# A two-block image network on one core: which engine takes the positive part and which the square, a second buffer of weighed values, and one form of samples

## The reference

```
x = x + mixer(ln(x))     # sim = relu(xn xn^T) ** 2 over all 3136 tokens; y = sim (x W)
t = t + experts(ln(t))   # 16 experts, the best two of each token, softmax shares
x = x + deformed(ln(x))  # 9 taps; each reads 4 corner rows at positions computed from x; then a 576 -> 64 product
t = t + routed_ffn(ln(t))# the 1567 tokens of largest routing weight get an FFN, weighted
```

## Time and profile before

| | us |
|---|---|
| median of 3 runs | 4409.18 (4400.55 to 4422.35) |
| profiled execution, its own time | 4427.31 |
| its span, first to last instruction | 4425.5 |
| GpSimd busy, in 2608 instructions | 2925.6 |
| TensorE / VectorE / ScalarE busy | 2910.2 / 2435.6 / 1761.2 |

### The profile page before, as it was taken

How to read it: one execution, slowest core, us unless ns; L and a number is a source line. 1 busy time by engine, 2 the same in 40 slices (tenths; PEclk the granted TensorE clock), 3 DMA queues, 4 the chain that set the end, 5 groups by cost and what they waited for, 6 DMA issues and landing times.

```text
span 4425.5 us, 51603 instructions
## 1 busy us (share of the span) xinstructions
PE 2910.2 (66%) x17810; PEld 1891.5 (43%) x17810; DVE 2435.6 (55%) x3747; ACT 1761.2 (40%) x2959; POOL 2925.6 (66%) x2608
## 2 busy tenths in 40 slices
PE   5969687586757786777777676788681357146432
PEld 2434534452446345633465345633460146135321
DVE  6354454744675456655665466655654245345775
ACT  5656466245523562355425552365231112122210
POOL 0040074777777776777767777777777777776770
PEclk8979798678856895678667886589665556555555
DMA  5000214321533132423342144313351325243446
GB/s 123 8 15 9 39 24 102 100 77 50 127 96 96 39 106 82 131 54 97 85 116 77 51 110 111 110 33 107 87 133 47 104 88 131 62 127 91 121 111 120
DMA packets 540746, 375.76 MB, mean 85 GB/s; under 512 B 465872, under 2 KB 470736, under 8 KB 540496
## 3 DMA queue, kind: packets, MB, share of 16 engines
q0 software_dynamic: 110848, 257.07, 20.1%
q1 hardware_dynamic: 429648, 115.40, 12.5%
HBM read 308.79 MB, written 89.41 MB: 90 GB/s over the span
## 4 chain that ended last, share of the span: by engine, by line
POOL 43%; PE 23%; issue 13%; DVE 11%; ACT 4%; DMA 3%; DVEq 2%; SPq 1%; ACTq 0%; POOLq 0%
POOL G L548 28%; PE PS L1689 22%; POOL shared L562 9%; POOL slot_rows L554 6%; DVE G L623 2%; DMA G<-corner_table,index 2%; DVE G L629 1%; DMA out<-experts_w 1%; DVEq L625 1%; DVE small L972 1%; DVE value L631 1%; PE PS L1724 1%; DVE st L590 1%; ACT small L1551 0%; DVE smallc L590 0%
## 5 line engine op out<-in xcount | busy, mean ns | idle before, releaser
L548 POOL DMA_INDIRECT G<-corner_table,index x1800 | 2029.3, 1127 | 681.6 <-issue 537.0
L623 DVE TENSOR_TENSOR G<-G,corner_w 128x768 f32<-128x768 f32 x600 | 541.5, 953 | 678.2 <-DMA G<-corner_table,index 678.1
L1515 ACT ACTIVATE work<-PS 128x768 f32<-128x768 f32 (+2 forms) x800 | 643.2, 822 | 541.9 <-PE PS L1689 277.8
L1689 PE MATMUL PS<-xn 128*128 128x400 f16 (+3 forms) x3200 | 647.9, 346 | 236.0 <-ACT work L1515 229.8
L951 DVE TENSOR_TENSOR work<-work 128x768 f32<-128x768 f32 (+2 forms) x496 | 479.7, 973 | 457.0 <-PE PS L1689 415.3
L554 POOL DMA_INDIRECT slot_rows<-split_a,slot x400 | 485.1, 1213 | 335.1 <-DVE slot L1046 213.5
L562 POOL DMA_INDIRECT shared<-slot_results,slot x400 | 410.1, 1025 | 349.5 <-DMA slot_results<-shared 227.8
L1689 PE MATMUL PS<-work,xm 128*64 128x400 f32 (+3 forms) x3200 | 638.0, 517 | 0.0
L1689 PEld LDWEIGHTS PS<-xn 128*128 128x128 f16 (+1 forms) x3200 | 289.8, 101 | 666.4 <-ACT work L1515 389.2
L1724 PE MATMUL PS<-ident,value 128*128 128x128 f32 x800 | 181.8, 370 | 522.3 <-DVE xq L636 275.5
L1423 ACT ACTIVATE val_cm<-PS 128x512 f32<-128x512 f32 x200 | 119.1, 596 | 694.5 <-PE PS L1724 694.3
(11 more groups left out here) (266 smaller groups left out, 3591.7 us busy)
## 6 DMA issues: line engine op xcount, KB each, us to landing
G<-corner_table,index POOLq DMA_INDIRECT x1800
corner_table<-rows_scratch SPq DMA_DIRECT2D x32, 784.0 KB
shared<-slot_rows SPq DMA_DIRECT2D x32, 512.0 KB, 7.6
slot_results<-shared SPq DMA_DIRECT2D x32, 512.0 KB
corner_table<-G SPq DMA_DIRECT2D x8, 841.0 KB, 10.5
slot_rows<-split_a,slot POOLq DMA_INDIRECT x400
shared<-slot_results,slot POOLq DMA_INDIRECT x400
experts_w<-x_scratch SPq DMA_DIRECT2D x8, 784.0 KB, 6.2
```

What stands on the lines that cost most here:

```text
L548: GP.indirect_dma_start(G[0:rows, n % 2, tap * 4 * C:(tap + 1) * 4 * C], None, tables[b % 2], bass.IndirectOffsetOnAxis(ap=index[0:rows, c ...
L623: V.tensor_tensor(g, g, bc(w, 2, C), ALU.mult)
L1515: A.activation(relu[0:rows, u % 2, :, 0:n], PS[u % 2][0:rows, :, 0:n], ACT.Relu).then_inc(s["relu_done"], 1)
L1689: return P.matmul(o, a, b, start=start, stop=stop, skip_group_check=True)
```

## The change

In five of eight mixer steps (1, 2, 4, 5, 7) VectorE now takes the positive part, out of PSUM, and ScalarE squares in all eight; ScalarE keeps the positive part in steps 0, 3, 6. The similarities of step u+2 wait for the positive part of step u on whichever engine makes it; the positive part of step u waits for the square of step u-2 (two buffers `relu`, as before). `value` gets a second buffer. The weighing of turn 0 (tile 23) stands ahead of the second half's wait for `y_done`. All samples have token form; `ident2`, its two loads, `dcn_cm` and line 1429 go. In `ffn_down` the two halves of the routing weight are two columns of one product, added in `ffn_bias`. `sel` and `eq16` are views of other tiles. The core of the diff:

```diff
-MIX_SAMPLE, MIX_EVAC, MIX_ADD, MIX_WEIGH = (0, 2, 4, 6), (1, 3, 5), 7, (2, 3, 4, 6, 7)
+MIX_SAMPLE, MIX_EVAC, MIX_ADD, MIX_WEIGH = (0, 2, 4), (1, 3), 7, (2, 3, 4, 6, 7)
...
-            loads = [(ident2[0:C, :], ident_in[0:C, 0:C]), (ident2[C:128, :], ident_in[0:C, 0:C]),
-                     (rank[:, :], rank_in[0:1, :].to_broadcast([TP, E])), (w_mix[:, :], conv_w),
+            loads = [(rank[:, :], rank_in[0:1, :].to_broadcast([TP, E])), (w_mix[:, :], conv_w),
...
-                    if piece == 4 and b * T + t > 0:
-                        dve.wait_ge(s["val_tr"], 2 * (b * T + t))
+                    if piece == 4 and b * T + t > 1:
+                        dve.wait_ge(s["val_tr"], 2 * (b * T + t - 1))
...
-                                dve.wait_ge(s["relu_done"], g + u + 1)
-                                free = squares_taken(hn, g + u)
-                                if free > 0:
-                                    dve.wait_ge(s["mixed"], free)
-                                V.tensor_tensor(sq[0:rows, u % 4, :, 0:n], relu[0:rows, u % 2, :, 0:n], relu[0:rows, u % 2, :, 0:n],
-                                                ALU.mult).then_inc(s["sq_dve"], 1)
+                                dve.wait_ge(s["sim_done"], g + u + 1)
+                                if g + u > 1:
+                                    dve.wait_ge(s["squared"], g + u - 1)
+                                V.tensor_scalar(relu[0:rows, u % 2, :, 0:n], PS[u % 2][0:rows, :, 0:n], 0.0, None,
+                                                ALU.max).then_inc(s["relu_dve"], 1)
...
+                    if half:
+                        turn_weighing(k, 0)
...
-                    V.tensor_scalar(w, Y1[0:RP, 448:448 + RT], descale[0:RP, ROUTE:ROUTE + 1], brc[:, 0:1], ALU.mult, ALU.add)
+                    red(w, Y1[0:RP, 448:448 + 2 * RT].rearrange("p (t two) -> p t two", two=2))
+                    dve.drain()
+                    V.tensor_scalar(w, w, descale[0:RP, ROUTE:ROUTE + 1], brc[:, 0:1], ALU.mult, ALU.add)
...
+            def square_step(s_no, half, jh, u):
...
+                if u in DVE_STEPS:
+                    act.wait_ge(s["relu_dve"], relus_dve(hn, jh, u))
                 else:
-                    act.wait_ge(s["sq_act"], square_act(hn, jh, u))
+                    act.wait_ge(s["relu_act"], relus_act(hn, jh, u))
+                free = squares_taken(hn, s_no)
+                if free > 0:
+                    act.wait_ge(s["mixed"], free)
+                A.activation(sq[0:rows, u % 4, :, 0:n], relu[0:rows, u % 2, :, 0:n], ACT.Square).then_inc(s["squared"], 1)
...
+                            if u + 1 in ACT_STEPS and u + 1 < steps(jh):
                                 if u:
-                                    squared(hn, jh, u - 1)
-                                elif jh:
-                                    squared(hn, jh - 1, SPB - 1)
+                                    act.wait_ge(s["squared"], g + u)
                                 relu_step(g + u + 1, half, jh, u + 1)
...
+                            if u == SPB - 1:
+                                act.wait_ge(s["squared"], g + u)
+                                relu_step(g + SPB, half, jh + 1, 0)
+                            square_step(g + u, half, jh, u)
                             beside_mixer(k, j, u)
...
-                                    pe.wait_ge(s["relu_done"], g + u + 1)
+                                    wait_relu(hn, jh, u)
                                     sims(half, jh * JB + (u + 2) // 2, u)
...
-                        for w in (wrh, wrl):
-                            ins = mm(Y1[0:RP, 448 + t:449 + t], xf[:, t * RP:(t + 1) * RP], w[:, 0:1], w is wrh, w is wrl)
+                        ins = mm(Y1[0:RP, 448 + 2 * t:450 + 2 * t], xf[:, t * RP:(t + 1) * RP], wr2[:, :])
```

## The result

| | before | after |
|---|---|---|
| median, us | 4417.51 (10 runs, 4400.55 to 4440.85) | 4375.59 (10 runs, 4360.96 to 4391.68) |
| ratio | 1 | 0.9903 (0.9883 to 0.9923) |
| profiled execution, span | 4425.5 | 4382.6 |

The change makes the kernel 1.0% faster. The forecast was 4338 us, 71 us less than the 4409 us known then; measured are 42 us less (43 between the two profiled spans). By the ratio, 0.9903 x 4409.18 = 4366 us, which is in the forecast range and nearly what rival A gave (4368).

The account below looks back on a forecast made before the run. GpSimd's indirect DMAs were taken to set the pace, held up by VectorE instructions with two SBUF inputs. 73.7 + 1.2 + 1.1 - 5 = 71 us gained, 4409 - 71 = 4338 us; range 4300 to 4400.

Parts of the forecast that it names:

- rival A: Mixer, units 3 to 7: VectorE makes tile 23 late, GpSimd rests 6 us a unit; 30 us back, 4368; chance 0.13.
- likeliest case: Whole kernel: main forecast of 71 us gained, 4338 us, own range 4318 to 4362; chance 0.64.
- signs of being wrong: Maxima holding GpSimd up, GpSimd's rests growing at tiles 23 to 1, or TensorE idle after step 7 in unit 0.
- main term: Units 3 to 7, 154 early GpSimd instructions: without VectorE's squares, busy as in unit 8; 73.7 us gained, 14.7 a unit.
- The maximum's duration: VectorE's positive part from PSUM in the mixer: 0.97 us each, load unchanged; bounds 0.62 and 1.06 us.
- The ring: Mixer step 7's positive part waits for step 5's square on ScalarE: 0.15 us a body, 5 us in units 0 to 2.
- Rival B: Mixer, step 7: 1.9 us lost a body, 98 us against 76 gained, 4431; decides from 1.6 us a body; chance 0.06.
- GpSimd 14 us earlier pulls the mixer with it: Mixers of units 3 to 7: mixer moves with GpSimd, since VectorE waits for gathers in its second half; 2.7 us cover.
- The moved weighing: Turn 0, tile 23 ahead of `y_done`: nothing for the path, 3 us more cover; up to 15 if the mixer lags.
- Small terms: Two loads fewer at the start 1.1 us, routing weight columns in unit 9 1.2 us; token form and second value buffer 0.
- Rival C: Early stretch: long GpSimd instructions have another cause or the maximum holds too; 2.3 us gained, 4407; chance 0.11.
- Rival D: Turns before the routing result: faster TensorE FFN shortens four rests too, at most 62 us; half gives 4307; chance 0.06.

Follow-up runs that it names:

- experiment 1: Changed kernel with the squares of five steps back on VectorE and all positive parts back on ScalarE; 4412.3 us, ratio 0.9968.
- experiment 7: Changed kernel with the maximum as a two-input operation, similarities in PSUM and zeros in SBUF instead of a constant; 4363.22 us (one run).
- experiment 8: Kernel of experiment 1 with its five VectorE squares replaced by a doubling with a constant, one SBUF input; 4384.42 us (one run).
- experiment 5: Changed kernel with six buffers squared in place instead of two for positive parts and four for squares; 4373.74 us, ratio 0.9913.
- experiment 9: Changed kernel with two VectorE waits inside the mixer (GpSimd's results, ScalarE's offsets) moved behind later maxima; 4367.11 us, ratio 0.9896.
- experiment 3: Changed kernel with tile 24's weighing moved into turn 0, ahead of tile 23's sample addition and the rest of the normalization; 4367.66 us, ratio 0.9876.
- experiment 6: Changed kernel with three weighings (tile 24's, those of turns 6 and 7) one turn earlier in VectorE's order; 4356.48 us, ratio 0.9867.
- experiment 2: Changed kernel with the weighing of turn 0 (tile 23) back behind the wait for y_done, two value buffers kept; 4397.67 us, ratio 0.9942.
- experiment 12: Kernel of experiment 2 with one buffer of weighed values, the last piece waiting for the tile before; 4403.53 us, ratio 0.9978.
- experiment 10: Changed kernel with the edits of experiment 6 and experiment 9 together; 4345.2 us, ratio 0.9843.
- experiment 11: Kernel of experiment 10 with the six buffers squared in place of experiment 5; 4344.25 us, ratio 0.9844.

## Why the prediction was right, and where 29 us of it went

The time lies in the stated range, 4300 to 4400, but not where the main forecast had it: 4375.6 us by the medians, 4366 by the ratio, against 4318 to 4362 as the likeliest case's own range. (The terms named for that range, added up, give 4309 to 4376.) What happened behind GpSimd's release is nearest to rival A (the mixer does not keep up with GpSimd), which had 0.13; the range held A as well, and that the prediction came out right by it is in part luck. One of its own signs of being wrong came true: GpSimd's rests grew between tiles 23 and 1.

**The cause was right.** VectorE with two SBUF inputs holds an indirect DMA up; with its one input in PSUM, or one of two, it does not (after, experiments 1 and 7). The trace of experiment 1 beside that of the change is the same code but for the swap. Two SBUF inputs are not the whole condition: the doubling of experiment 8 has one, and holds. The Trainium skill, SBUF — State Buffer, section "Who interferes with whom", infers that tensor_tensor would leave descriptor generation alone; experiment 1's 877.5 us against 818.1 disagree, at least for these DMAs, whose addresses are read from a tile; whether the reading of the addresses or the generation is held was not separated. Its other rule there, that an instruction with at most one SBUF input does not contend outside the two-port modes, agrees with experiment 7's 823.2 us; whether experiment 8's doubling, which holds with one SBUF input, ran in such a mode no run here shows.

**The size of the main term, 73.7 us, was 11 too large.** The same subtraction now gives 62.5. Units 3 to 7 still stand 818.07 - 5 x 160.79 = 14.1 us above unit 8 with no square left in them. The term was mis-sized because unit 8 differs from the others by more than the squares, and all of the difference was put down to them. The trace before shows it: in units 3 to 7 174 DMAs start while a square is under way, and they are 64 us longer in sum than DMAs beside which VectorE does nothing; after, 157 start under a maximum and are 0.3 us longer in sum. The other 9 or 10 us are DMAs that start under VectorE's other instructions. Of GpSimd's 78.9 us the remaining 16 lie elsewhere: 9 in unit 2 (its first 154 instructions sum to 170.1 us before and 161.0 after), where GpSimd waits for the mixer anyway.

**The maximum's duration** was taken as 0.97 us: 971 ns. VectorE's load stayed, 2431.0 us against 2435.6.

**The ring, 5 us lost in units 0 to 2**: a bare body is 11.5 us instead of 11.4, so the ring loses 0.1 us a body where 0.15 was taken. A loss of 7 us is there in unit 2, but not by the ring. Experiment 5 takes the ring away and the loss stays; experiment 9 moves two waits of VectorE and it goes. Rival B's pace of 1.6 us a body did not come; the bare mixer still keeps TensorE busy. Lengths and busy times of the engines in the stretch of the earlier trace rows, after:

```profile
60.00:126.00 66.00, 65.98 (x371) 26.93 (x370) 25.89 (x28) 49.84 (x64) 0.00 (x0) 1.00 0.43 106
```

**"GpSimd 14 us earlier pulls the mixer with it" is the step that failed.** In unit 5 the last square of the mixer started 226.7 us after the first gather of results; the last maximum starts 221.5 us after it. The mixer came 5 us earlier, GpSimd 13: from the first gather of results to the next image's first tile it is 235.7 us, before 248.9. For tile 23 the forecast had named the cover, 2.7 us and 3 us of the moved weighing. For what comes next it took cover that was not there: "the tiles of the first three turns wait for their gathers, the first 5.79 us". The 5.79 us stand ahead of the third of these tiles, the next image's first. Tile 24, the second, is weighed from 2159.95 to 2164.91 us behind the normalization, without a wait for gathers, and GpSimd needs it at 2170.61. VectorE and then GpSimd, before:

```profile
2159.95 2.69 DVE L623 TENSOR_TENSOR G<-G,corner_w 128x768 f32<-128x768 f32 x3
```

```profile
2170.61 0.95 POOL L548 DMA_INDIRECT G<-corner_table,index  x1 [0.30 <-issue]
```

So the cover at tile 24 was 5.7 us (3.2 to 5.7 over units 3 to 7), and GpSimd used it up. That is rival A's effect, at the tile after the one it named: 21.0 us of rests where A had 30. From the first gather of results of unit 3 to that of unit 8 it is 2389.4 us before and 2336.9 after: 10.5 us a unit, where 14 were forecast. Experiment 3 takes these rests away and gains 8 us by the medians; experiment 6 also takes away those ahead of the routing, and gains 19.

**The moved weighing**, priced at nothing "if the mixer follows" and at up to 15 us if not, is worth 17 to 22 us with the swap (experiment 2): the condition came true. What it is worth without the swap was not tried; in experiment 1 it delays the addition by 7 us.

**Small terms.** The 1.1 us of two loads fewer cannot be seen: the first gather of results starts at 547.85 us before, at 547.76 after, and between 545.25 and 551.76 in the experiments. GpSimd's rest in unit 9 is 18.66 us before, 17.86 after and 17.11 to 18.50 in the experiments, all of which have the routing weight as two columns: 0.2 to 1.5 us for 1.2. Token form was not tried by itself, and the second buffer of `value`, taken at nothing, is not settled by experiment 12.

**Rival C** is excluded by the stretches. **Rival D** did not come in the profiled execution: the rests ahead of the routing result are 15.29, 15.29, 7.83 and 5.21 us after, 15.53, 15.52, 7.83 and 5.20 before; but they vary from trace to trace (last section).

## What to carry to other kernels

When one engine sets the pace because another holds it up, price the release by the instructions that start under the holder, not by a stage that lacks it. Here that gives 64 us where the stage gave 73.7 and 62.5 came; it is not exact either, for in experiment 1 the same sum is 51 us of an excess of 59.4. And follow the first two or three things that the faster engine will wait for, for the gain ends at the first that does not move with it. When an operation that frees a buffer moves to an engine with a long hand-written order, every blocking wait in that order now stands ahead of the release. Here the order of a few weighings and of two waits was worth another 30 us by the medians (4375.6 to 4345.2) and 0.60% by the ratios, beside 42 us and 0.97% for the change itself.

The largest holder is still there. After the change the DMAs that start while a weighing is under way (lines 615, 621 and 623, two SBUF inputs each) are 270 us longer in sum than DMAs beside which VectorE does nothing, more than four times what the swap released. No run tried to take that away.

## What the runs showed of the hardware that was not expected

The rest ahead of the routing result lasts from 5.2 to 15.3 us in one execution of the same code. TensorE's granted clock in the 26 us before the routing's wait ends differs: after the change it is 0.51 and 0.52 in units 4 and 5 (rests of 15.29 us) and 0.84 and 0.81 in units 6 and 7 (7.83 and 5.21 us). The eleven traces that have the weighings ahead of the routing in their old places (all but experiments 6, 10 and 11) agree: 15 rests of 13 us and more at 0.50 to 0.52, 29 shorter ones at 0.55 to 0.91. Unit 5 after (rest 15.29), and unit 5 in experiment 1, where the turns are the same (rest 5.32); length, busy of PE, PEld, DVE, ACT, POOL, clock:

```profile
2186.30:2212.30 26.00, 24.95 (x123) 20.21 (x122) 14.59 (x29) 5.23 (x9) 20.41 (x19) 0.52 0.32 96
```

```profile
2195.60:2221.60 26.00, 21.13 (x158) 17.14 (x156) 19.11 (x35) 6.67 (x12) 20.82 (x18) 0.89 0.29 86
```

At 0.52 (nearly all at the lower level, 1.2 GHz) TensorE is busy throughout and VectorE waits for it; at 0.89 (most of it at the upper, 2.4 GHz) it is done earlier. Which of the two a unit gets differs from trace to trace; no kernel was profiled twice, so whether it differs between executions of one kernel is not shown. It matters when single profiles are compared: these four rests sum to 43.6 us after the change, 30.3 in experiment 3 and 31.9 in experiment 9, where the medians are smaller gains than the profiled executions show. What TensorE did before the clock rose in the one and not in the other was not followed.
